# Gated cross-attention and expert block on one core: first inversion split, ids, shares and cells of the second batch reordered

## The chip, the cores and the metric

The kernel runs on one core of a Trainium2 chip. The core has TensorE (PE, matrix products into PSUM), VectorE (DVE), ScalarE (ACT), GpSimd (POOL) and SyncE (SP, which issues DMAs). Each runs its own instruction stream in order and waits for the others on semaphores. The metric is the time of one execution in microseconds (us). Three runs took 621.59, 623.06 and 623.34 us.

## The reference, cut to what matters

`x` is (2, 2048, 512), two batches of 2048 tokens; `ctx` is (2, 154, 512).

```
x = x + tanh(g_xattn) * align(ctx, layernorm(x))      # x1
x = x + tanh(g_ffn)   * experts(layernorm(x1))

align(small, large):            # per batch
    D = euclidean distances (154 x 2048)
    R = cost of the cheapest monotone path through D (dynamic time warping)
    walk back along the path; every cell (i, j) adds small[i] to row j

experts(xf):                    # 8 experts, 512 x 512 each, the best 2 per token
    logits = xf @ gate_w.T
    w, sel = top_k(logits, 2);  w = softmax(w)
    out[n] = sum over the 2 chosen e of  w * (xf[n] @ expert_w[e])
```

## The kernel before, in words

The first 240 us find the path: distances, cost recursion and the walk back, whose end is VectorE work alone. From then on tokens are handled in tiles of 128: 32 tiles, 16 for each batch (`TB` is 16, `t` counts tiles, tile 16 is the first of the second batch).

For each batch the path becomes a 0/1 matrix `prow`, context rows by tokens. `cells(b, half)` makes half of its columns on VectorE: two operations that hold the tick numbers between the limits of a row (line 963), then two compares (line 968); whatever is passed as `between` stands between them. `gated(t)` on TensorE (lines 1606, 1608) multiplies it with small tables for the gate logits of a tile, all 16 tiles into PSUM bank 6. `align(t)` (lines 1621, 1623) multiplies it with the context rows in three bf16 pieces, one PSUM bank per tile, and `add_context(t)` on VectorE (line 985) adds the result to the token tile, which gives x1. The banks go round: alignment of tile 20 needs the bank that `add_context(18)` empties.

`choose(b)` on VectorE (lines 1000 to 1023) takes the two best experts of every token of the batch from bank 6, after all 16 `gated`. `count(b)` on TensorE (lines 1629, 1630) counts them, and `place_choices(b)` on VectorE (from line 1029) gives each of the 4096 choices a slot in 39 tiles (`JT`) that belong to one expert each. The slots are inverted on TensorE, from token by slot to slot by token: `lay_lanes` and `lay_numbers` on VectorE lay two one-hot operands (lines 1068, 1079, 1080), `pads(b)` adds operands for the unused places of the last tile of every expert (lines 1087 to 1097), and `invert(b)` runs 32 matmuls on the first two (line 1643) and 9 on the pads (line 1647). `ids(b)` copies the result into lists of row numbers, for gathers and for the adding DMAs at the end (lines 1126, 1127). `rank(b)` (line 1635) is a small product that `pads` reads. `own_tiles(b)` lays each tile's expert.

ScalarE meanwhile makes `centred(t)`, the x1 rows less their mean, line 1364, which SyncE stores to DRAM as `x2` (line 489) from a ring of four buffers, and `squares(t)`, the sum of squares of the tile, line 1350, with a read of the accumulator. `root(b)` (line 1356) takes the root of the variance for the batch after its 16 squares; `scales(b)` on VectorE (lines 992, 993) needs it, and gives the difference of the logits, from which ScalarE's `shares(b)` takes the exponential (line 1373). Between the two ScalarE copies a set of operands, `members_turned(b)` (line 1368). `lay_shares(b)` on VectorE waits for both (lines 1104 to 1119), `invert_shares(b)` on TensorE (line 1657) inverts the shares to tiles, and `shares_by_tile(b)` on VectorE (line 1132) reads them out.

The expert loop then takes 78 gathered tiles in the order `SEQ`: GpSimd gathers 128 rows (line 637), TensorE transposes them (`turn`, line 1679), ScalarE copies the transposes (`copy_in`, line 1393), TensorE multiplies with the expert's matrix (`expert`, line 1694), ScalarE scales the result (`copy_out`, line 1403) and GpSimd adds it to the output in DRAM (line 650). The first 11 are of batch 0; during them TensorE also runs the alignment of the rest of batch 1, `count(1)`, `rank(1)` and `invert(1)`, and VectorE the whole placement of batch 1. The order on every engine is written out by hand.

Of the kernel before, what the change touches and what calls it, by code (L numbers as in the profile page):

```python
# [5 lines left out]
ALU = mybir.AluOpType  # L6
# [3 lines left out]
F16 = mybir.dt.float16  # L10
# [4 lines left out]
P = 128  # L15
# [4 lines left out]
def flamingo_block(nc, x_d, ctx_d, gx_d, gf_d, gate_d, exp_d, out_d):  # L20
    B, T, C = x_d.shape
    S = ctx_d.shape[1]
    E = gate_d.shape[0]
    CH = C // P
    NT = B * T // P
# [36 lines left out]
    TB = NT // B  # L62
    KT = K * TB
# [22 lines left out]
    with ExitStack() as ctx:  # L86
# [3 lines left out]
        def sem(name):  # L90
            return ctx.enter_context(nc.semaphore(name))
# [270 lines left out]
        s_outside = sem("outside_last_tiles")  # L362
        s_rank = sem("outside_ranked")
        s_oneh = sem("slots_one_hot")
        s_inv = sem("slots_inverted")
        s_ids = sem("tile_ids")
        s_shareh = sem("shares_laid")
# [52 lines left out]
        ALIGNED = [[], [18, 19], [20, 21, 22], [23, 24, 25], [26, 27, 28], [29, 30, 31]]  # L420
        LATE = (4, 5, 4, 5, 4, 5, 6, 4, 5, 6, 4, 5, 6, 4, 5, 6)
        COUNTS = (7, 6)

        def bank(t):
            return RING[t % AR] if t < TB else LATE[t - TB]
# [248 lines left out]
        def _(v):  # L674
# [280 lines left out]
            def cells(b, half, between=lambda: None):  # L955

                n = 2 * (2 * b + half)
                cols = slice(half * HT, (half + 1) * HT)
                low, high = limits[:, half, 0, :, :], limits[:, half, 1, :, :]
                for k in range(2):  # L960
                    if n:
                        v.wait_ge(s_p, n + k - 1)
                    v.tensor_scalar(held[:, k, :], ticks[:, :], low[:, k, b:b + 1], high[:, k, b:b + 1],
                                    ALU.max, ALU.min).then_inc(s_held, 1)
                between()
                for k, rows in enumerate((pmain, prest)):
                    v.wait_ge(s_held, n + k + 1)
                    v.tensor_tensor(rows[:, b, cols], held[:, k, :], ticks[:, :], ALU.is_equal).then_inc(s_p, 1)
# [6 lines left out]
            def lnk(ins):  # L975
                ln[0] += 1
                ins.then_inc(s_gt, 1)
                v.wait_ge(s_gt, ln[0])
# [9 lines left out]
            def scales(b):  # L988

                ts = slice(b * TB, (b + 1) * TB)  # L990
                v.wait_ge(s_sd2, b + 1)
                lnk(v.reciprocal(rs2[:, ts], sd2[:, ts]))
                v.tensor_tensor(sc[:, 0, ts], sc[:, 0, ts], rs2[:, ts], ALU.mult).then_inc(s_dif, 1)
# [76 lines left out]
            def lay_numbers(b):  # L1070

                sets = sets_of(b)
                member = sets[:, SETS - 1, :, :]
                if b:
                    for g in (2, 3):
                        v.wait_ge(s_out[g], 16)
                    v.wait_ge(s_xn2, TB)
                    v.wait_ge(s_sq, TB)
                lnk(v.tensor_tensor(member, spread(partf[:, 0, 0:1], [[0, JT], [1, KT]]), tilen[:, :, :], ALU.is_equal))
                v.tensor_tensor(sets[:, 0, :, :].bitcast(F16), member, spread(numbers[:, 0, 0:1], [[0, JT], [1, KT]]),  # L1080
                                ALU.mult)

            def pads(b):

                v.wait_ge(s_rank, b + 1)
                place_e = padpos[:, 0:E]
                lnk(v.scalar_tensor_tensor(place_e, ntl, -float(P), spread(upto[:, KT - 1:KT], [[KT, E]]),
                                           ALU.mult, ALU.add))
                lnk(v.scalar_tensor_tensor(place_e, place_e, float(P), psum[:, 7, 2 * P:2 * P + E], ALU.add, ALU.add))
                v.tensor_copy(padpos[:, E:LAST], lane[:, :])  # L1090
                lnk(v.scalar_tensor_tensor(place_e, inl[:, :], float(2 * P), place_e, ALU.mult, ALU.add))
                for e in range(LAST):
                    v.tensor_scalar(padhot[:, e, :], stripe[:, :], padpos[:, e:e + 1], None, ALU.is_equal)
                v.tensor_tensor(padset[:, 0:E, :], spread(lastt[:, 0:1], [[1, E], [0, JT]]),
                                spread(tiles[:, 0:1], [[0, E], [1, JT]]), ALU.is_equal)
                lnk(v.tensor_scalar(padset[:, E, :], tiles[:, :], tend[:, E - 1:E], None, ALU.is_ge))
                v.tensor_scalar(padset[:, :, :], padset[:, :, :], lane[:, 0:1], None, ALU.mult).then_inc(s_oneh, 1)

            def lay_shares(b):

                ts = slice(b * TB, (b + 1) * TB)
                sets = sets_of(b)
                v.wait_ge(s_gte, b + 1)
                lnk(v.tensor_scalar(sc[:, 2, ts], sc[:, 1, ts], 1.0, None, ALU.add))
                lnk(v.reciprocal(sc[:, 3, ts], sc[:, 2, ts]))
                lnk(v.scalar_tensor_tensor(share[:, 0, ts], sc[:, 3, ts], tgates[:, 1:2], rs2[:, ts],
                                           ALU.mult, ALU.mult))
                lnk(v.tensor_tensor(share[:, 1, ts], sc[:, 1, ts], share[:, 0, ts], ALU.mult))
                part = share[:, :, ts]
                split = [pieces[:, m, :].rearrange("p (k t) -> p k t", k=K) for m in range(3)]  # L1110
                left = [rests[:, m, :].rearrange("p (k t) -> p k t", k=K) for m in range(2)]
                lnk(v.tensor_copy(split[0], part))
                lnk(v.tensor_tensor(left[0], part, split[0], ALU.subtract))
                lnk(v.tensor_copy(split[1], left[0]))
                lnk(v.tensor_tensor(left[1], left[0], split[1], ALU.subtract))
                lnk(v.tensor_copy(split[2], left[1]))
                v.wait_ge(s_mem, b + 1)
                for m in range(PARTS):
                    ins = v.tensor_tensor(by_slot(sets)[:, :, m, :], members_by_slot(b),
                                          spread(pieces[:, m, 0:1], [[1, KT], [0, JT]]), ALU.mult)  # L1120
                ins.then_inc(s_shareh, 1)

            def ids(b):

                v.wait_ge(s_inv, b + 1)
                v.tensor_copy(gids[:, b, :], psum[:, 7, 0:JT])
                v.tensor_scalar(aids[:, b, :], psum[:, 7, 0:JT], float(b * T), None, ALU.add).then_inc(s_ids, 1)
# [16 lines left out]
                add_context(t)  # L1144
            pads(0)
            own_tiles(0)
            cells(1, 0, lambda: (ids(0), scales(0)))
            cells(1, 1)
            lay_shares(0)
            choose(1, lambda: shares_by_tile(0))  # L1150
            for t in (16, 17):
                add_context(t)
            place_choices(1)
# [20 lines left out]
        def _(act):  # L1174
# [200 lines left out]
            for t in range(10):  # L1375
                centred(t)
                squares(t)
            for t in range(10, TB, 2):
                centred(t)
                centred(t + 1)  # L1380
                if t < TB - 2:
                    squares(10 + (t - 10) // 2)
            for t in range(12, TB):
                squares(t)
            root(0)
            members_turned(0)
# [38 lines left out]
        def _(pe):  # L1425
# [206 lines left out]

            def rank(b):
                pe.wait_ge(s_outside, b + 1)
                nc.tensor.matmul(psum[:, 7, 2 * P:2 * P + E], earlier[:, :], outside[:, :],
                                 start=True, stop=True).then_inc(s_rank, 1)

            def invert(b):

                pe.wait_ge(s_oneh, b + 1)  # L1640
                sets = sets_of(b)
                for i in range(KT):
                    ins = nc.tensor.matmul(psum[:, 7, 0:JT], lanes[:, :, i], sets[:, 0, :, i].bitcast(F16),
                                           start=(i == 0), stop=(i == KT - 1))
                    if i == 0:
                        for e in range(LAST):
                            nc.tensor.matmul(psum[:, 7, 0:JT], padhot[:, e, :], padset[:, e, :],
                                             start=False, stop=False)
                ins.then_inc(s_inv, 1)

            def invert_shares(b):
# [47 lines left out]
            pe.wait_ge(s_x1, TB)  # L1699
            align(16)  # L1700
            align(17)
            for t in range(TB + TB // 2, NT):
                gated(t)
            turn(0)
            for n in range(NSEQ):
                own = owned(n)
                if n + 1 < NSEQ:
                    turn(n + 1)
                expert(n, own)
                if n == 0:  # L1710
                    invert_shares(0)
                if n == 1:
                    count(1)
                if n == 5:
                    invert(1)
                if n < len(ALIGNED):
                    for t in ALIGNED[n]:
                        align(t)
                if n == 2:
                    rank(1)  # L1720
                if n == 10:
                    invert_shares(1)
# [26 lines left out]
```

## Time and profile before

| | |
|---|---|
| median of 3 runs | 623.06 us |
| the profiled execution's own time | 623.45 us |
| its span, first to last instruction | 621.6 us |
| mean granted clock of TensorE, of full | 0.87 |
| TensorE matmul busy | 468.9 us (75%) |
| VectorE busy | 286.5 us (46%) |
| ScalarE busy | 241.4 us (39%) |
| GpSimd busy | 237.3 us (38%) |

The busy shares are means over very different stages. VectorE is nearly full up to 300 us and mostly idle later; TensorE is nearly idle from 172 to 243 us and full from 290 us to the end. The change sits where the one passes into the other, between 270 and 310 us.

### The profile page before, as it was taken

The page shows a single profiled execution, that of the slowest core. Times are in us where ns is not written, and L with a number is a line of the kernel's source. Part 1 is how long each engine was busy: PE and PEld are TensorE (multiplying, and loading weights), DVE is VectorE, ACT ScalarE, POOL GpSimd, SP SyncE. Part 2 cuts the span into 40 slices and gives each one's busy share as a digit, 9 for nine tenths or more (in the row PEclk, how much of TensorE's full clock was granted, in tenths as well). Part 3 has the DMA queues.
Part 4 walks back from the last instruction along what each step waited for, and adds up shares of the span by engine and source line. Part 5 has one row for each costly group of instructions (what it writes and reads, how often), then busy time and mean ns, then how long its engine had stood idle before and what let it go on. Part 6 is the DMA issues. An engine that isn't in the chain of part 4 may idle for free.

```text
span 621.6 us, 7820 instructions
## 1 busy us (share of the span) xinstructions
PE 468.9 (75%) x2118; PEld 276.3 (44%) x2118; DVE 286.5 (46%) x1522; ACT 241.4 (39%) x449; POOL 237.3 (38%) x228
## 2 busy tenths in 40 slices
PE   5999667567100001828999999999999999999994
PEld 5999644344100001315445544444444444444441
DVE  4878989999988885999861400000000000000000
ACT  4477685444400000484779322222222333333331
POOL 5900230000000000004432456676567667666853
PEclk9899877977555555776999999999999999999998
DMA  8962269710051004376878957787787778678875
GB/s 253 391 221 74 70 153 251 188 27 1 0 202 69 1 1 141 124 283 214 272 191 245 283 98 134 136 160 135 120 162 133 134 141 153 113 140 153 147 125 67
DMA packets 56108, 91.78 MB, mean 148 GB/s; under 512 B 19263, under 2 KB 19263, under 8 KB 55907
## 3 DMA queue, kind: packets, MB, share of 16 engines
q0 software_dynamic: 18016, 43.00, 37.5%
q1 hardware_dynamic: 33523, 39.88, 19.5%
q10 hardware_dynamic: 4528, 8.41, 4.2%
q8 instruction: 19, 0.31, 0.2%
q14 instruction: 22, 0.18, 0.1%
HBM read 50.05 MB, written 41.21 MB: 147 GB/s over the span
## 4 chain that ended last, share of the span: by engine, by line
PE 59%; DVE 31%; DMA 4%; issue 4%; ACT 1%; POOL 0%; SPq 0%; POOLq 0%; ACTq 0%; DVEq 0%
PE psum L1694 40%; DVE met L923 5%; PE psum L1679 5%; PE psum L1472 5%; DVE waves L836 5%; DVE tokens L926 3%; DVE tokens L861 3%; DVE shf L827 2%; PE psum L1459 2%; DVE tokens L839 2%; DVE tokens L985 2%; PE psum L1621 2%; DVE tokens L830 2%; DMA ar<-in_ctx_dram 1%; DVE waves L826 1%
## 5 line engine op out<-in xcount | busy, mean ns | idle before, releaser
L1694 PE MATMUL psum<-big,tokens 128*128 x624 | 280.6, 593 | 0.3 <-ACT tokens L1393 0.3
L1694 PEld LDWEIGHTS psum<-big,tokens 128*128 128x128 f32 x624 | 112.5, 190 | 112.9 <-issue 112.9
L637 POOL DMA_INDIRECT tokens<-x_rows,gather_ids x78 | 79.1, 1014 | 45.7 <-issue 21.3
L650 POOL DMA_INDIRECT out_dram<-work,add_ids x40 | 63.2, 1580 | 53.6 <-DMA out_dram<-work,add_ids 26.3
L650 POOL DMA_INDIRECT out_dram<-prow,add_ids x38 | 59.9, 1577 | 45.9 <-DMA out_dram<-prow,add_ids 11.9
L657 POOL DMA_DIRECT2D out_dram<-tokens x2 | 1.8, 912 | 172.3 <-DVE tokens L985 172.3
L1403 ACT ACTIVATE work<-psum,tile_shares 128x512 f32<-128x512 f32 x40 | 27.5, 686 | 99.4 <-PE psum L1694 93.5
L1403 ACT ACTIVATE prow<-psum,tile_shares 128x512 f32<-128x512 f32 x38 | 26.1, 686 | 92.1 <-PE psum L1694 92.1
L1364 ACT ACTIVATE stage<-tokens,nm 128x512 f32<-128x512 f32 x32 | 21.7, 713 | 96.8 <-DVE tokens L985 96.7
L1679 PEld LDWEIGHTS psum<-ident,tokens 128*128 128x128 f32 x312 | 39.0, 143 | 39.0 <-issue 33.7
L1590 PE MATMUL psum<-side,work 128*128 128x2 f32 x8 | 1.9, 356 | 70.9 <-DVE work L944 70.9
L1393 ACT COPY tokens<-psum 128x512 f32<-128x512 f32 x78 | 45.0, 579 | 12.2 <-PE psum L1679 12.2
L1679 PE MATMUL psum<-ident,tokens 128*128 128x128 f32 x312 | 47.3, 275 | 1.3 <-DMA tokens<-x_rows,gather_ids 1.3
L836 DVE TENSOR_TENSOR_SCAN waves<-waves,shf,tokens 128x65 f32<-128x65 f32 x108 | 37.9, 351 | 2.4 <-DMA tokens<-dist_rows 2.4
L1472 PE MATMUL psum<-aT,big 128*128 128x162 f32 x256 | 37.7, 305 | 0.0
L1472 PEld LDWEIGHTS psum<-aT,big 128*128 128x128 f32 x256 | 36.6, 194 | 0.0
L1590 PEld LDWEIGHTS psum<-side,work 128*128 128x128 f32 x8 | 1.8, 327 | 71.0 <-DVE work L944 71.0
L923 DVE SCALAR_TENSOR_TENSOR met<-tokens 128x70 bf16<-128x70 bf16 x108 | 31.5, 292 | 3.8
L1621 PE MATMUL psum<-sm,prow 128*128 128x512 bf16 x96 | 29.1, 415 | 1.4 <-DVE tokens L985 1.4
L826 DVE TENSOR_TENSOR waves<-waves 128x64 f32<-128x64 f32 x108 | 24.3, 225 | 0.1
L985 DVE SCALAR_TENSOR_TENSOR tokens<-psum,tgates,tokens 128x512 f32<-128x512 f32 x32 | 22.3, 743 | 2.5 <-PE psum L1623 2.1
L1350 ACT ACTIVATE aT<-tokens,nm 128x512 f32<-128x512 f32 x32 | 23.0, 719 | 1.1
(320 smaller groups left out, 614.2 us busy)
## 6 DMA issues: line engine op xcount, KB each, us to landing
tokens<-in_x_dram SPq DMA_DIRECT2D x16, 1024.0 KB, 11.1
stage<-in_L_ffn_expert_w_dram ACTq DMA_DIRECT2D x8, 1024.0 KB, 6.2
x_rows<-stage SPq DMA_DIRECT2D x32, 256.0 KB, 2.5
out_dram<-tokens SPq DMA_DIRECT2D x6, 1024.0 KB, 8.1
tokens<-dist_rows SPq DMA_DIRECT2D x52, 64.0 KB, 2.2
dist_rows<-work SPq DMA_DIRECT2D x16, 160.0 KB, 2.0
out_dram<-tokens POOLq DMA_DIRECT2D x2, 1024.0 KB, 5.1
dist_rows<-prow SPq DMA_DIRECT2D x5, 256.0 KB, 10.4
```

Of the source, the lines that this page charges most:

```text
L637: pool.indirect_dma_start(out=xin[:, n % UX, :], out_offset=None, in_=x2_d[b][:, :], in_offset=bass.IndirectOffsetOnAxis(ap=gids[:, b, j:j ...
L650: pool.indirect_dma_start(out=out_d.rearrange("b t c -> (b t) c"), in_=yout(n), in_offset=None, out_offset=bass.IndirectOffsetOnAxis(ap=ai ...
L826: v.tensor_tensor(mring[:, s % 3, 1:W1], up[:, 0:W], up[:, 1:W1], ALU.min).then_inc(s_min, 1)
L836: v.tensor_tensor_scan(own, mring[:, s % 3, :], dring[:, s // CS % DR, s % CS, :], shf[:, s % 2, 0:1], ALU.min, ALU.add).then_inc(s_row, 1)
L923: v.scalar_tensor_tensor(met[:, :], words[:, s + 1, :], words[:, s + 1, TW - 1:TW], itab[:, s, :], ALU.is_equal, ALU.mult, accum_out=words ...
L985: v.scalar_tensor_tensor(x[:, t, :], psum[:, bank(t), :], tgates[:, 0:1], x[:, t, :], ALU.mult, ALU.add).then_inc(s_x1, 1)
L1393: nc.scalar.copy(xinT[:, n % UX, :, :].rearrange("p c n -> p (c n)"), psum[:, n % UP, :]).then_inc(s_yc, 1)
L1403: nc.scalar.mul(yout(n), psum[:, UP + n % UP, :], scale[:, b, j:j + 1]).then_inc(s_ye, 1)
L1472: ins = nc.tensor.matmul(to, xT[:, c, at + k * P:at + (k + 1) * P], aT[:, b, c, :], start=(c == 0), stop=(c == CH - 1))
L1621: nc.tensor.matmul(psum[:, bank(t), :], pmain[:, b, cols], sm[:, b, j, 0:C], start=(j == 0), stop=False)
L1679: ins = nc.tensor.transpose(psum[:, n % UP, c * P:(c + 1) * P], xin[:, n % UX, c * P:(c + 1) * P], ident[:, :])
L1694: ins = nc.tensor.matmul(psum[:, UP + n % UP, :], xinT[:, n % UX, c, :], expT[:, bass.ds(own, 1), c, :].rearrange("p o d -> p (o d)"), sta ...
```

## The change

- `invert(b)`: the 32 matmuls on the slot numbers come first, on a new semaphore that `lay_numbers` raises; the 9 on the pads come last, in batch 0 behind their own wait.
- `rank(0)` writes to bank 6 beside the gating results instead of to bank 7.
- VectorE: `ids(0)` ahead of `cells(1, 0)` instead of inside it; `lay_shares(0)` ahead of `cells(1, 1)`; `shares_by_tile(0)` ahead of `choose(1)` instead of inside it.
- ScalarE: `centred` of tiles 10 to 15, then `squares` of tiles 10 to 15, instead of the two interleaved.
- TensorE: `gated` of tiles 24 to 31 behind expert 0 and `invert_shares(0)` instead of ahead of the first transposes.

```diff
+        RANKS = ((6, 3 * G * TB), (7, 2 * P))
...
                 v.tensor_tensor(sets[:, 0, :, :].bitcast(F16), member, spread(numbers[:, 0, 0:1], [[0, JT], [1, KT]]),
-                                ALU.mult)
+                                ALU.mult).then_inc(s_numl, 1)
...
             pads(0)
             own_tiles(0)
-            cells(1, 0, lambda: (ids(0), scales(0)))
+            ids(0)
+            cells(1, 0, lambda: scales(0))
+            lay_shares(0)
             cells(1, 1)
-            lay_shares(0)
-            choose(1, lambda: shares_by_tile(0))
+            shares_by_tile(0)
+            choose(1)
...
-            for t in range(10, TB, 2):
+            for t in range(10, TB):
                 centred(t)
-                centred(t + 1)
-                if t < TB - 2:
-                    squares(10 + (t - 10) // 2)
-            for t in range(12, TB):
+            for t in range(10, TB):
                 squares(t)
...
             def invert(b):
 
-                pe.wait_ge(s_oneh, b + 1)
+                pe.wait_ge(s_numl, b + 1)
+                if b:
+                    pe.wait_ge(s_oneh, b + 1)
                 sets = sets_of(b)
                 for i in range(KT):
-                    ins = nc.tensor.matmul(psum[:, 7, 0:JT], lanes[:, :, i], sets[:, 0, :, i].bitcast(F16),
-                                           start=(i == 0), stop=(i == KT - 1))
-                    if i == 0:
-                        for e in range(LAST):
-                            nc.tensor.matmul(psum[:, 7, 0:JT], padhot[:, e, :], padset[:, e, :],
-                                             start=False, stop=False)
+                    nc.tensor.matmul(psum[:, 7, 0:JT], lanes[:, :, i], sets[:, 0, :, i].bitcast(F16),
+                                     start=(i == 0), stop=False)
+                if b == 0:
+                    pe.wait_ge(s_oneh, 1)
+                for e in range(LAST):
+                    ins = nc.tensor.matmul(psum[:, 7, 0:JT], padhot[:, e, :], padset[:, e, :],
+                                           start=False, stop=(e == LAST - 1))
                 ins.then_inc(s_inv, 1)
...
             align(16)
             align(17)
-            for t in range(TB + TB // 2, NT):
-                gated(t)
             turn(0)
             for n in range(NSEQ):
...
                 if n == 0:
                     invert_shares(0)
+                    for t in range(TB + TB // 2, NT):
+                        gated(t)
```

On VectorE, from the owners of batch 0 (`am`, `owners`) on, the order before was this; `work` are the held ticks and `prow` the cells, `rs` and `sc` belong to `scales(0)`, and the `sc` row at the end begins `lay_shares(0)`.

```order
L1062 CAST owners<-am 1x39
L963 TENSOR_SCALAR work<-ticks,row_limits 128x1024 x2
L1126 CAST gather_ids<-psum 128x39
L1127 TENSOR_SCALAR add_ids<-psum 128x39
L992 RECIPROCAL rs<-aux 128x16
L993 TENSOR_TENSOR sc<-sc,rs 128x16
L968 TENSOR_TENSOR prow<-work,ticks 128x1024 x2
L963 TENSOR_SCALAR work<-ticks,row_limits 128x1024 x2
L968 TENSOR_TENSOR prow<-work,ticks 128x1024 x2
L1104 TENSOR_SCALAR sc<-sc 128x16
```

It is now as follows; the lines below the edits have moved by 2.

```order
L1064 CAST owners<-am 1x39
L1128 CAST gather_ids<-psum 128x39
L1129 TENSOR_SCALAR add_ids<-psum 128x39
L965 TENSOR_SCALAR work<-ticks,row_limits 128x1024 x2
L994 RECIPROCAL rs<-aux 128x16
L995 TENSOR_TENSOR sc<-sc,rs 128x16
L970 TENSOR_TENSOR prow<-work,ticks 128x1024 x2
L1106 TENSOR_SCALAR sc<-sc 128x16
```

The ids have moved ahead of the held ticks, and the second pair of held ticks and cells no longer stands between the first and the shares. Where it stands now shows further down the same engine, at the end of `lay_shares(0)` (`ar`, `tokens`) and the start of `choose(1)` (`ar<-psum`, line 1002 now):

```order
L1118 CAST ar<-ar 128x32
L1121 TENSOR_TENSOR tokens<-tokens,ar 128x32x39 x3
L965 TENSOR_SCALAR work<-ticks,row_limits 128x1024 x2
L970 TENSOR_TENSOR prow<-work,ticks 128x1024 x2
L1134 TENSOR_REDUCE tile_shares<-psum 128x39
L1002 TENSOR_REDUCE ar<-psum 128x144
```

Between the shares and `choose(1)` there are now the second half of the cells and the tile shares. On TensorE, around the end of expert 0 (`big` are the experts' matrices) and the inversion of the shares (32 matmuls), the order before was

```order
L1694 MATMUL psum<-big,tokens 128x512
L1657 MATMUL psum<-tokens,stage 128x117 x32
L1687 TENSOR_LOAD owners
L1687 ISA x2
L1679 MATMUL psum<-ident,tokens 128x128 x4
```

and it is now, with the first two of the eight moved tiles:

```order
L1698 MATMUL psum<-big,tokens 128x512
L1661 MATMUL psum<-tokens,stage 128x117 x32
L1607 MATMUL psum<-sm,prow 128x27
L1609 MATMUL psum<-srs,prow 128x9
L1607 MATMUL psum<-sm,prow 128x27
```

The gating of tiles 24 to 31 follows the shares' inversion, where the next tile's transposes stood.

## Rows read from the trace of the kernel before

**Rows 1.** The page's chain that ended last: shares of the span by engine.

```profile
PE 59%; DVE 31%; DMA 4%; issue 4%; ACT 1%; POOL 0%; SPq 0%; POOLq 0%; ACTq 0%; DVEq 0%
```

**Rows 2.** TensorE's waits, 268 to 350 us: total us, times, longest us.

```profile
PE psum L1643 <- DVE waves L1097: 9.1, 1, 9.1
```

**Rows 3.** The chain in order of time, 280 to 400 us: start us, us, what.

```profile
286.09 1.28 PE psum L1621 x3
287.37 0.43 PE psum L1623
...
288.20 0.97 PE psum L1679 x4
...
289.92 3.69 PE psum L1694 x8
293.61 2.01 PE psum L1657 x32
...
305.55 0.66 DVE tokens L985
```

**Rows 4.** Timeline of VectorE: start us, us, instruction, [idle before, releaser].

```profile
271.96 4.04 DVE L985 SCALAR_TENSOR_TENSOR tokens<-psum,tgates,tokens 128x512 f32<-128x512 f32 x6
...
280.26 0.98 DVE L963 TENSOR_SCALAR work<-ticks,row_limits 128x1024 f16<-128x1024 f16 x2
281.80 0.20 DVE L1126 CAST gather_ids<-psum 128x39 uint32<-128x39 f32 x1 [0.55 <-PE psum L1643]
...
282.39 1.33 DVE L968 TENSOR_TENSOR prow<-work,ticks 128x1024 bf16<-128x1024 f16 x2
...
285.80 0.29 DVE L1104 TENSOR_SCALAR sc<-sc 128x16 f32<-128x16 f32 x1
...
292.10 0.60 DVE L1000 TENSOR_REDUCE ar<-psum 128x144 f32<-128x432 f32 x1
...
295.73 0.28 DVE L1132 TENSOR_REDUCE tile_shares<-psum 128x39 f32<-128x117 f32 x1 [0.28 <-PE psum L1657]
...
299.76 0.69 DVE L1029 TENSOR_TENSOR_SCAN am<-aT,psum 128x256 f32<-128x256 f32 x1 [0.56 <-PE psum L1630]
```

**Rows 5.** Timeline of ScalarE, squares to exponential of batch 0.

```profile
277.88 0.71 ACT L1350 ACTIVATE aT<-tokens,nm 128x512 f32<-128x512 f32 x1
...
280.60 0.74 ACT L1350 ACTIVATE aT<-tokens,nm 128x512 f32<-128x512 f32 x1
...
281.47 0.31 ACT L1356 ACTIVATE aux<-inverse_roots,eps 128x16 f32<-128x16 f32 x1
281.69 2.32 ACT L1368 COPY tokens<-tokens 128x1248 bf16<-128x1248 bf16 x1
284.02 1.28 ACT L1373 ACT_TABLE_LOAD   x1
285.32 0.21 ACT L1373 ACTIVATE sc<-sc 128x16 f32<-128x16 f32 x1
```

**Rows 6.** Timeline of TensorE at the inversion and at two waits.

```profile
279.15 0.48 PE L1647 MATMUL psum<-waves 128*128 128x39 f16 x9
279.47 2.29 PE L1643 MATMUL psum<-tokens,stage 128*128 128x39 f16 x31
...
306.26 0.82 PE L1621 MATMUL psum<-sm,prow 128*128 128x512 bf16 x3 [0.92 <-DVE tokens L985]
...
347.83 0.66 PE L1679 MATMUL psum<-ident,tokens 128*128 128x128 f32 x4 [1.35 <-DMA tokens<-x_rows,gather_ids]
```

**Rows 7.** Windows of 1 us: sum, five engines' busy us, PEclk, DMA share, GB/s.

```profile
280.00:281.00 1.00, 1.00 (x18) 1.00 (x17) 0.97 (x4) 0.91 (x3) 0.00 (x0) 0.50 0.07 16
...
289.00:290.00 1.00, 0.69 (x6) 0.46 (x4) 1.00 (x2) 0.81 (x2) 0.57 (x1) 0.97 0.81 307
```

**Rows 8.** GpSimd's first gather; stores of x1 rows (line 489), issue to landing.

```profile
282.39 1.06 POOL L637 DMA_INDIRECT tokens<-x_rows,gather_ids  x1 [14.32 <-DVE add_ids L1127]
...
DMA to landing us min/median/max: 2.0/2.5/8.4
```

More of the change, by code:

```diff
@@ L364, in flamingo_block @@
         s_oneh = sem("slots_one_hot")
+        s_numl = sem("slot_numbers_laid")
         s_inv = sem("slots_inverted")
@@ L1088, in pads @@
                                            ALU.mult, ALU.add))
-                lnk(v.scalar_tensor_tensor(place_e, place_e, float(P), psum[:, 7, 2 * P:2 * P + E], ALU.add, ALU.add))
+                lnk(v.scalar_tensor_tensor(place_e, place_e, float(P), psum[:, RANKS[b][0], RANKS[b][1]:RANKS[b][1] + E], ALU.add, ALU.add))
                 v.tensor_copy(padpos[:, E:LAST], lane[:, :])
@@ L1634, in rank @@
                 pe.wait_ge(s_outside, b + 1)
-                nc.tensor.matmul(psum[:, 7, 2 * P:2 * P + E], earlier[:, :], outside[:, :],
+                nc.tensor.matmul(psum[:, RANKS[b][0], RANKS[b][1]:RANKS[b][1] + E], earlier[:, :], outside[:, :],
                                  start=True, stop=True).then_inc(s_rank, 1)
             def invert(b):
-                pe.wait_ge(s_oneh, b + 1)
+                pe.wait_ge(s_numl, b + 1)
+                if b:
+                    pe.wait_ge(s_oneh, b + 1)
                 sets = sets_of(b)
                 for i in range(KT):
-                    ins = nc.tensor.matmul(psum[:, 7, 0:JT], lanes[:, :, i], sets[:, 0, :, i].bitcast(F16),
-                                           start=(i == 0), stop=(i == KT - 1))
-                    if i == 0:
-                        for e in range(LAST):
-                            nc.tensor.matmul(psum[:, 7, 0:JT], padhot[:, e, :], padset[:, e, :],
-                                             start=False, stop=False)
+                    nc.tensor.matmul(psum[:, 7, 0:JT], lanes[:, :, i], sets[:, 0, :, i].bitcast(F16),
[5 more added lines that the diff above has]
+                                           start=False, stop=(e == LAST - 1))
                 ins.then_inc(s_inv, 1)
```

## The prediction

> **What bounds the kernel now.** I read the page's chain of waits first: TensorE is 59% of it, VectorE 31% [rows 1]. Then TensorE's own waits from 268 to 350 us: the longest, 9.1 us, is for the pads of the first inversion [rows 2]; the others of note are for the path cells of the second batch, 0.92 us for a token sum and 1.35 us for a gathered tile, which ends at 347.83 us [rows 6]. Behind that one TensorE has no wait up to its last matmul. So the change is worth what it moves TensorE's work at 347.83, and what sets that time comes down the chain in order of time [rows 3]: alignment of tiles 16 and 17, the transposes of gathered tile 0, expert 0, the inversion of the shares, and at 305.55 the sum of token tile 18 on VectorE. The last one matters most. Tile 20's alignment takes the PSUM bank that `add_context(18)` empties, and VectorE came to that sum only after `choose(1)`, the sums of 16 and 17 and `place_choices(1)`. There is no slack there: TensorE stood 0.92 us for it [rows 6].
>
> **The change, part by part.**
>
> *1. Inversion split (TensorE).* The 32 matmuls of the first inversion now need only the slot numbers, laid when the sums of tiles 10 to 15 begin, 271.96 [rows 4]; the 9 on the pads come last. Before, one ran, then the 9 in 0.48 us, then 31 in 2.29 us, to 281.76 [rows 6]. Now the 32 lie beside `add_context(10..15)`, and behind the pads (laid at 279.0) only the 9 remain. The inversion is ready at about 279.6 and VectorE finds it done when it comes to `ids(0)`.
>
> *2. `ids(0)` ahead of the held cells.* VectorE ends the owners at 280.26, does both ids in 0.31 us (281.80 to the end at 282.11 before), and holds the cells for 1.0 us, to 281.55. Its idle 0.55 us ahead of the ids goes [rows 4]. The gather of tile 0 starts at 280.57 + 0.28 = 280.85 instead of 282.39 [rows 8]. TensorE never waited for that gather, so on the path this brings nothing.
>
> *3. Six centred tiles first, six squares last (ScalarE).* The root of the x1 variance, on which `scales(0)` waits, comes after the last square. Before, two of the six squares of tiles 10 to 15 lay between centred tiles, and the last four ran at (280.60 - 277.88) / 3 = 0.907 us each, since each waits for the accumulator of the one before; the root started at 281.47 [rows 5]. Now all six do: 5.44 us. They start when `centred(15)` ends. That one waits for `add_context(15)`, done at 271.96 + 4.04 = 276.00, and for the store of tile 11, whose row buffer it takes: tile 11 is centred by about 274.05, and a store lands 2.0 us at the least and 2.5 us in the median after its issue [rows 8]. So it starts between 276.1 and 276.7, ends at 276.7 to 277.3, and the root starts at 282.2 to 282.8. I take 282.25, nearest to the row of VectorE's own pace: 0.8 us later than before.
>
> *4. Cells of the second batch, first half.* VectorE has held them by 281.55 and stands for the root, which ends at 282.25 + 0.31 = 282.56. From the reciprocal to the end of both compares it took 1.70 us (282.02 to 282.39, and 1.33) [rows 4]; so the cells are done at 284.35 instead of 283.72. Gating of tiles 16 to 23 starts 0.63 us late, and alignment of 17 ends at 287.80 + 0.63 = 288.43 [rows 3]. The 2.2 us of inversion taken off the path buy nothing: the squares on ScalarE take its place.
>
> *5. Gating of tiles 24 to 31 behind expert 0.* It filled the 0.40 us between alignment 17 and the transposes of tile 0 (287.80 to 288.20). So these start at 288.43, 0.23 us later than before, and expert 0 at about 290.15 instead of 289.92. Its 3.69 us and the 2.01 us of the share inversion [rows 3] end at 295.85.
>
> *6. `lay_shares(0)` ahead of `cells(1,1)`.* It waits for ScalarE's exponentials. Behind the root lie there the copy of the members (281.69 to 284.02, 2.33 us), a table load of 1.28 and the exponential, 0.21 [rows 5]; so they come at 286.3. Before, VectorE worked on the second half of the cells meanwhile; that cover is gone, and it is idle from 284.35 to 286.35. Then the shares take their 6.3 us (285.80 to 292.10) [rows 4]: laid at about 292.7. TensorE comes for them at 293.84, so the 2.0 us cost nothing there. `cells(1,1)` (1.0 and 1.3 us, 0.1 of it overlapped) ends at 294.9; TensorE runs the last gating matmuls from 295.85 to 296.3.
>
> *7. What is late next: `choose(1)`.* It reads all 16 gating results of the batch. Before, it started at 292.10, during expert 0, right behind the shares. Now it starts at 296.4, behind expert 0, the share inversion and the gating: 4.3 us later. From its start to the end of `add_context(18)` VectorE took 306.21 - 292.10 = 14.11 us [rows 3, 4]. Of this 0.48 us goes (the tile shares with the 0.28 us wait for them now come ahead), and so does the 0.56 us wait for the counting matmuls [rows 4], since TensorE does `count(1)` while VectorE adds 16 and 17. Left: 13.07 us. Tile 18 is added at 309.5 and the alignment of tile 20 starts at 309.52 instead of 306.26: **+3.26 us**. TensorE's own work up to there would be done by about 308, after new waits of about 1.3 us before the count and 0.5 us before alignment 18; so VectorE's chain decides and leaves 1.4 us idle before tile 20.
>
> *8. Behind that.* From tile 20 to the gather wait TensorE has the same work. The gather wait itself (1.35 us) ends with the stores of the second batch's rows, which follow ScalarE's `centred(31)`, which follows TensorE's alignment of 31: it moves along and absorbs nothing. The pads last in the second inversion: 41 matmuls as before. `rank(0)` in another PSUM bank: nothing.
>
> The sum against the profiled execution: 623.45 + 3.3 = 626.7, of which the span is 621.6 + 3.3 = 624.9. The median of the runs shown, 623.06, is 0.4 below that execution, so I forecast **626.4**.
>
> **The clock.** The granted clock was at its low level (0.50, 1.2 of 2.4 GHz) while the inversion ran at 280, and at the high one from 289, in the first transposes [rows 7]. At the low level an alignment took 1.28 + 0.43 = 1.71 us [rows 3], its first three matmuls 1.3 against 0.7 to 0.8 us later on [rows 6]. I expect the same two slow alignments, 16 and 17. If the rise comes only inside expert 0, up to 1 us is added, with half of expert 0's 3.4 us slow as the far bound of 1.7; if a little earlier than before, 0.5 us is saved.
> The Trainium skill (TensorE: Matmul & The Clock Gate, Part 1: The HAM clock gate) has it that activity releases the throttle and idleness brings it back. By that rule the inversion, moved to 272 right behind the alignments, might keep the engine at full clock. The trace speaks against it here: an inversion of the same length was followed by gating and alignment at 0.50. As a gain the rule is rival C.
>
> **Rivals.**
>
> *B, not slower.* The chain of VectorE behind `choose(1)` is hidden by experts 1 and 2, and the root is not late. Then the cells end at 281.55 + 1.70 = 283.25 (0.47 us earlier), the gating is out of the way (0.40), and TensorE's order alone counts: -0.9 us, 622.2. It decides from the point where VectorE has more than 4 us of slack between `choose(1)` and tile 18. Against it: the 0.92 us wait says that the slack is below zero. For it: only that TensorE was busy for all but 0.92 us of that stretch.
>
> *C, the clock stays high* through alignment 16 and 17. It saves 2 x 0.85 and half of the 0.97 us of transposes, 2.2 us, and leaves +1.1: 624.2. Against it: between the early inversion and the cells TensorE does nothing in some 10 us but the 9 pad matmuls.
>
> *D, later still.* The store of tile 11 lands late (the slowest of its line took 8.4 us [rows 8]), or the clock rises inside expert 0, or ScalarE, which now meets `centred(16)` only at 302.3 and has the second lane numbers behind it, holds up the copies that the experts need. +3.3 and 1.5 to 2 more: 628.2.
>
> **Chances.** A, the forecast, 0.67, with its own range 625.4 to 627.4 (the root 0.7 to 1.3 us late, the clock term 0.5 us either way, half the spread of the runs, 621.59 to 623.34). B 0.11, C 0.08, D 0.14. The measurement can tell some 0.3%, 1.9 us, from no change. Slower by more than that: nearly all of A, and D: 0.80. Within it: most of B and C, 0.15. Faster needs a gain of 1.9 us, twice that of B: 0.05. The range leaves out B and the far end of D: 623.5 to 628.4.
>
> **What would show it.** The 32 matmuls at 272; the root at 282.2 or later, VectorE waiting for it and then 2 us for the exponentials; expert 0 within 0.5 us of 290.1; `choose(1)` at about 296.4; new waits of TensorE before the count and alignment 18, and one of over 1 us before tile 20, which starts 3.3 us later; the gather wait still near 1.35 us. I am wrong if tile 20's alignment does not wait, if expert 0 starts more than 2 us earlier, or if the gather wait shrinks to nothing.

## The result and the profile after

The changed kernel took 626.32 us (median of 5 runs, 624.19 to 628.69), the kernel before 622.86 us beside it (median of 5, 621.59 to 623.34): 1.006 times as long, 95% interval 1.003 to 1.0089. It is slower by 3.46 us. The profiled execution took 626.32 us with a span of 624.6 us, against 621.6 us.

The two traces are laid over each other where the sums of tiles 10 to 15 begin on VectorE: 271.96 us before [rows 4], 272.00 us after. That matters, because in the traces of this study this point lies anywhere between 269.54 and 273.84 us, though nothing that VectorE does ahead of it was edited. Below, "after the origin" means this point of the same trace.

The chain of waits by engine, first row of the page's part on it:

```profile
PE 58%; DVE 33%; DMA 3%; issue 3%; ACT 2%; POOL 0%; SPq 0%; ACTq 0%; DVEq 0%; POOLq 0%
```

VectorE's share rose from 31% to 33% and ScalarE's from 1% to 2% [rows 1]. TensorE's timeline (start us, us, instruction, idle before and its releaser) shows where:

```profile
272.13 2.39 PE L1646 MATMUL psum<-tokens,stage 128*128 128x39 f16 x32 [2.09 <-DVE tokens L1082]
...
279.11 0.48 PE L1651 MATMUL psum<-waves 128*128 128x39 f16 x9 [4.59 <-DVE waves L1099]
...
285.40 0.20 PE L1607 MATMUL psum<-sm,prow 128*128 128x27 bf16 x1 [5.80 <-DVE prow L970]
...
287.51 1.32 PE L1622 MATMUL psum<-sm,prow 128*128 128x512 bf16 x3
...
290.26 3.70 PE L1698 MATMUL psum<-big,tokens 128*128 x8 [0.32 <-ACT tokens L1394]
...
301.54 0.28 PE L1630 MATMUL psum<-hot,earlier 128*128 128x256 bf16 x1 [0.75 <-DVE hot L1016]
...
302.64 0.60 PE L1622 MATMUL psum<-sm,prow 128*128 128x512 bf16 x2 [0.71 <-DVE tokens L987]
...
309.65 0.82 PE L1622 MATMUL psum<-sm,prow 128*128 128x512 bf16 x3 [1.46 <-DVE tokens L987]
...
350.10 0.66 PE L1683 MATMUL psum<-ident,tokens 128*128 128x128 f32 x4 [0.25 <-DMA tokens<-x_rows,gather_ids]
...
354.60 2.25 PE L1661 MATMUL psum<-tokens,stage 128*128 128x117 bf16 x32 [0.41 <-DVE tokens L1121]
```

The inversion is done at 279.6 us, yet the first matmul of the second batch's gating still waits, 5.80 us, for the cells. Tile 20 (309.65) waits 1.46 us for a token sum instead of 0.92 [rows 6], and the late gathered tile waits only 0.25 us instead of 1.35 [rows 6]. VectorE's timeline says what it did with the time:

```profile
280.31 0.18 DVE L1128 CAST gather_ids<-psum 128x39 uint32<-128x39 f32 x1
...
280.52 0.98 DVE L965 TENSOR_SCALAR work<-ticks,row_limits 128x1024 f16<-128x1024 f16 x2
283.68 0.25 DVE L994 RECIPROCAL rs<-aux 128x16 f32<-128x16 f32 x1 [2.18 <-ACT aux L1360]
...
287.44 0.17 DVE L1106 TENSOR_SCALAR sc<-sc 128x16 f32<-128x16 f32 x1 [2.10 <-ACT sc L1377]
...
296.06 0.28 DVE L1134 TENSOR_REDUCE tile_shares<-psum 128x39 f32<-128x117 f32 x1 [0.23 <-PE psum L1661]
296.48 0.61 DVE L1002 TENSOR_REDUCE ar<-psum 128x144 f32<-128x432 f32 x1
```

The 0.55 us wait of [rows 4] became one of 2.18 us for the root, and 2.10 us for the exponentials joined it. `choose(1)` begins at 296.48 instead of 292.10 [rows 4]. ScalarE's timeline has the cause of the first:

```profile
276.44 0.72 ACT L1368 ACTIVATE stage<-tokens,nm 128x512 f32<-128x512 f32 x1 [0.97 <-DMA x_rows<-stage]
277.33 0.72 ACT L1368 ACTIVATE stage<-tokens,nm 128x512 f32<-128x512 f32 x1 [0.17 <-issue]
277.96 0.71 ACT L1354 ACTIVATE aT<-tokens,nm 128x512 f32<-128x512 f32 x1
...
283.34 0.31 ACT L1360 ACTIVATE aux<-inverse_roots,eps 128x16 f32<-128x16 f32 x1
```

Two causes meet here. All six squares now lie behind `centred(15)`, two more than before, at 0.91 us each. And `centred(14)` stood 0.97 us for the store of tile 10. So the six squares began at 277.96 and the root at 283.34, against 281.47 before [rows 5].

### The profile page after: what moved, and what is told of

Read it like the earlier page. It is cut to its first block, busy times and chain, and to the rows that moved or that the text cites. A ratio compares the mean times of both kernels' runs of the same rounds, so it can differ in the third digit from the quotient of the medians.

```text
span 624.6 us, 7808 instructions
## 1 busy us (share of the span) xinstructions
PE 468.7 (75%) x2106; PEld 277.8 (44%) x2118; DVE 286.6 (46%) x1522; ACT 242.1 (39%) x449; POOL 238.1 (38%) x228
## 4 chain that ended last, share of the span: by engine, by line
PE 58%; DVE 33%; DMA 3%; issue 3%; ACT 2%; POOL 0%; SPq 0%; ACTq 0%; DVEq 0%; POOLq 0%
PE psum L1698 41%; DVE met L925 5%; PE psum L1683 5%; PE psum L1473 5%; DVE waves L838 5%; DVE tokens L928 3%; DVE tokens L863 3%; DVE shf L829 2%; PE psum L1460 2%; DVE tokens L841 2%; DVE tokens L832 2%; PE psum L1622 2%; DMA ar<-in_ctx_dram 1%; DVE tokens L987 1%; DVE waves L828 1%
## 5 line engine op out<-in xcount | busy, mean ns | idle before, releaser
L1698 PE MATMUL psum<-big,tokens 128*128 x624 | 280.6, 593 | 0.3 <-ACT tokens L1394 0.3
L1622 PE MATMUL psum<-sm,prow 128*128 128x512 bf16 x90 | 27.2, 407 | 3.5 <-DVE tokens L987 2.9
```

Of the source, the lines that this page charges most:

```text
L1622: nc.tensor.matmul(psum[:, bank(t), :], pmain[:, b, cols], sm[:, b, j, 0:C], start=(j == 0), stop=False)
L1698: ins = nc.tensor.matmul(psum[:, UP + n % UP, :], xinT[:, n % UX, c, :], expT[:, bass.ds(own, 1), c, :].rearrange("p o d -> p (o d)"), sta ...
```

## The experiments

Every kernel was timed against the kernel before, in three sets of four kernels (e1 to e4; e5, e6, e7 and e10; e11 to e14), each with its own runs of the kernel before on the same chip (medians 623.73, 623.87 and 623.35 us). The runs of one kernel spread by 2 to 8 us, and the start of the stretch of interest alone moves by 4.3 us from trace to trace, so steps are read from one trace each, in us after the origin. "Gather ends" is where the transposes of gathered tile 11 begin, the tile that TensorE waits for in [rows 6]:

```
                                gating 16  expert 0  choose(1)  tile 20  gather   last matmul
                                starts     starts    starts     aligned  ends     ends
before                          11.82      17.96     20.14      34.30    75.87    341.00
after                           13.40      18.26     24.48      37.65    78.10    343.88
e1 gating late only             11.83      17.46     23.76      37.00    77.45    343.22
e2 after, ScalarE as before     11.56      17.05     23.21      36.28    76.74    342.49
e3 split and ids only           11.55      17.28     20.03      33.77    75.41    340.52
e4 e3 + squares last            13.26      19.06     21.49      35.34    77.00    342.15
e5 e3 + scales after cells      10.76      17.82     20.12      34.57    76.68    343.61
e6 after + sums in placing      13.57      18.34     24.65      36.21    77.06    342.82
e7 e5 + sums in placing         10.76      17.84     20.13      33.50    75.74    340.92
e10 before + sums in placing    11.83      17.97     20.16      33.25    75.19    340.34
e11 e3 + sums in placing        11.58      17.72     20.05      32.98    75.41    342.24
e12 e11 + twelve ahead          11.56      17.71     20.03      32.95    -        341.71
e13 e11 + nine idle matmuls     11.61      15.99     19.87      32.10    73.93    339.08
e14 before + twelve ahead       11.83      17.62     20.15      34.08    -        342.99
```

**One part done alone: the gating of tiles 24 to 31.** On the kernel before:

```diff
-            for t in range(TB + TB // 2, NT):
-                gated(t)
             turn(0)
...
                     invert_shares(0)
+                    for t in range(TB + TB // 2, NT):
+                        gated(t)
```

> One part alone: the gating of tiles 24 to 31 moved behind the inversion of the shares, all else as before. My theory (the decision chain of VectorE has no slack behind choose(1)): choose(1) starts at about 296.0 instead of 292.1, TensorE then waits over 1 us for the sum of tile 18, and the time is +2.6 to +3.4 us, about 626. The rival (the late root and the cells behind it cost the time, not the gating): -0.4 to 0, about 622.7.

Measured: 624.49 us, ratio 1.0013 (1.0 to 1.0026), some 0.8 us slower (0 to 1.6), where 2.6 to 3.4 had been expected. In the trace tile 20 is 2.70 us late and the last matmul 2.22 us. VectorE's timeline of this kernel, around `choose(1)`:

```profile
287.27 4.20 DVE L1119 TENSOR_TENSOR tokens<-tokens,ar 128x1248 bf16<-128x1248 bf16 x3
294.99 0.61 DVE L1000 TENSOR_REDUCE ar<-psum 128x144 f32<-128x432 f32 x1 [3.52 <-PE psum L1608]
```

VectorE had the shares laid and then stood 3.52 us for the last gating matmul. With this one edit step 7 of the prediction is there: `choose(1)` 3.6 us late, tile 20 2.7 us late. The size in the time was missed, and is less than the trace has it.

**One part undone: the squares.** The changed kernel with ScalarE's old order:

```diff
-            for t in range(10, TB):
-                centred(t)
-            for t in range(10, TB):
-                squares(t)
+            for t in range(10, TB, 2):
+                centred(t)
+                centred(t + 1)
+                if t < TB - 2:
+                    squares(10 + (t - 10) // 2)
+            for t in range(12, TB):
+                squares(t)
```

> The changed kernel with ScalarE's order as before (squares 10 and 11 between the centred tiles). Root back to about 281.5 from 283.3, cells of the first half at 283.5, expert 0 at about 289.1. My theory: choose(1) still starts only behind expert 0, the share inversion and the gating, at about 295.4, so +2.0 to +2.6 us against the kernel before, about 625.2. The rival (the late root carries the loss): within 0.5 us of the kernel before, 623.

Measured: 624.62 us, 1.0016 (1.0005 to 1.0028), 0.3 to 1.7 us slower than the kernel before, less than the 2.0 to 2.6 expected. Tile 20 comes 1.37 us earlier than in the changed kernel (36.28 for 37.65), the last matmul 1.39. So the late root is worth about 1.4 of the 3.35 us at tile 20. ScalarE never stood for a store here: its root began at 9.49 after the origin, against 11.34 in the changed kernel and 9.51 before. In all three traces with the squares last it stood, 0.97 us in the changed kernel, 0.81 in e4 and 1.13 in e6, and the root began at 11.34, 11.19 and 11.50.

**The parts without the late gating.** e3 keeps the inversion split and the ids first, with ScalarE's, TensorE's and VectorE's further order as before:

```diff
-            cells(1, 0, lambda: (ids(0), scales(0)))
+            ids(0)
+            cells(1, 0, lambda: scales(0))
```

> Only the split inversion and ids(0) ahead of the held cells; ScalarE, shares, cells and gating as before. My theory: VectorE's 0.55 us wait for the inversion goes and little more, since it then meets the root: -0.2 to -0.8 us, about 622.4. The rival (the inversion's 2.2 us were on the path and come off it): -2 us or more, under 621.

e4 is e3 with the squares last.

> As the split-and-ids kernel, with the six squares behind the six centred tiles as in the changed kernel; shares, cells and gating as before. My theory: the root comes 1.8 us later and VectorE, which has no slack, moves with it: choose(1) at about 293.5, +1.0 to +1.6 us against the kernel before, about 624.2. The rival (a late root hides behind the second half of the cells): as the split-and-ids kernel within 0.3 us.

Measured: e3 622.83 us, 0.9982 (0.9964 to 0.9999); e4 624.95 us, 1.001 (0.9991 to 1.0029). e3 came out as expected in size. VectorE no longer waits for the inversion there, and meets the root instead:

```profile
281.87 0.25 DVE L994 RECIPROCAL rs<-aux 128x16 f32<-128x16 f32 x1 [0.33 <-ACT aux L1359]
```

The split gains 0.53 us at tile 20 and 0.48 at the end: the root was right behind the inversion. The squares last turn this into 1.04 us later than before at tile 20 and 1.15 at the end (e4).

**Taking the root out of the way.** e5 is e3 with the reciprocal of the root behind the whole first half of the cells:

```diff
-            cells(1, 0, lambda: scales(0))
+            cells(1, 0)
+            scales(0)
```

> The split-and-ids kernel with scales(0) behind the two compares of cells(1,0) instead of ahead of them, so that the cells don't wait for the root. Counted from the end of lay_numbers(0): gating of tile 16 at 10.8 us instead of 11.8 in the kernel before, tile 20 at 33.5 instead of 34.3, last matmul at 340.2 instead of 341.0; -0.8 us. The rival (VectorE's chain has slack, TensorE's own order counts): -1.0 at the gating and at tile 20 alike, with the wait before tile 20 gone.

Measured: 624.94 us, 1.0018 (1.0001 to 1.0034): a miss, slower where a gain of 0.8 us was expected. The gating did start 1.06 us earlier than before, but expert 0 only 0.14 us, and `choose(1)` not at all. GpSimd's timeline of this kernel:

```profile
281.18 2.15 POOL L639 DMA_INDIRECT tokens<-x_rows,gather_ids  x1 [13.38 <-ACT aT L1354]
283.64 2.08 POOL L639 DMA_INDIRECT tokens<-x_rows,gather_ids  x1 [0.30 <-issue]
286.02 0.94 POOL L639 DMA_INDIRECT tokens<-x_rows,gather_ids  x1 [0.30 <-issue]
```

and TensorE's, at the transposes of gathered tile 0, and at tile 11:

```profile
288.18 0.66 PE L1686 MATMUL psum<-ident,tokens 128*128 128x128 f32 x4 [0.43 <-DMA tokens<-x_rows,gather_ids]
...
348.36 0.66 PE L1686 MATMUL psum<-ident,tokens 128*128 128x128 f32 x4 [1.92 <-DMA tokens<-x_rows,gather_ids]
348.85 5.30 PE L1701 MATMUL psum<-big,tokens 128*128 x8
```

Two gathers took 2.1 us of GpSimd instead of 1.06 [rows 8], and TensorE stood for the first of them. VectorE ran holds and compares beside them almost without a gap; but so it did in the kernel before, from 282.39 to 285.87, where the gathers took 1.06, 1.04 and 0.99 us. What made these two longer stays open. Later the expert of tile 11 took 5.30 us instead of 3.60, at a granted clock of 0.50 from 349 to 352 us.

**What waits at tile 20.** If `add_context(18)` comes too late, it can go ahead of the rest of `place_choices(1)`:

```diff
-            place_choices(1)
-            for t in (18, 19):
-                add_context(t)
+            place_choices(1, lambda: [add_context(t) for t in (18, 19)])
```

with the call of the function behind the line that computes `tbeg`. On the changed kernel:

> The changed kernel with add_context(18) and (19) inside place_choices(1), behind its tbeg, instead of behind it. If TensorE's wait of 1.46 us before tile 20 is VectorE's chain, it goes: tile 20 at 36.2 us from the end of lay_numbers(0) instead of 37.65, and the last matmul 0.3 to 1.1 us earlier than in the changed kernel, at 342.8 to 343.6. The rival (the wait hides another that takes its place, PSUM or the count): tile 20 at 37.5 or later.

on e5:

> The scales-after-cells kernel with the sums of tiles 18 and 19 inside place_choices(1) as well. Tile 20 without a wait at 32.4 us instead of 34.3 in the kernel before, tile 22 at 34.4 instead of 36.0, last matmul at 339.3 instead of 341.0: -1.7 us, about 622.0 where the kernel before takes 623.7. The rival (the later gather wait, 1.35 us before, grows by what is gained): last matmul at 340.2, no better than the kernel it is made from.

on the kernel before:

> The kernel before with only the sums of tiles 18 and 19 moved inside place_choices(1). Theory: the 0.92 us wait before tile 20 goes, tile 20 at 33.4 us from the end of lay_numbers(0), last matmul at 340.1 instead of 341.0: -0.9 us. The rival (absorbed by the gather wait): 341.0, no change.

and on e3:

> The split-and-ids kernel (-0.5 us in its trace) with the sums of tiles 18 and 19 inside place_choices(1) (-0.7 us in its trace). Both act on VectorE's one chain at different places, so they should add: last matmul at 339.8 us from the end of lay_numbers(0) instead of 341.0, -1.2 us. The rival (the gather wait of tile 11 takes back what is gained): 340.5.

Measured: e6 626.3 us, 1.0044 (1.0028 to 1.006); e7 624.15, 1.0002 (0.9984 to 1.0019); e10 622.88, 0.9991 (0.9974 to 1.0007); e11 623.09, 0.9985 (0.9965 to 1.0004). The wait ahead of tile 20 is gone in all four. In the changed kernel that gives 1.06 us in the trace, as expected, so the wait was real and no longer the only one: tile 22 waits 0.26 us. The time of e6 does not show this gain. In the kernel before it gives 0.66 us in the trace (0.9 expected) and nothing that the times can tell. e7 and e11 missed: their last matmuls ended at 340.92 and 342.24, later than even their rivals had it. e11 had 0.46 us in hand at the gather wait and then lost more than that:

```profile
345.87 1.12 PE L1684 MATMUL psum<-ident,tokens 128*128 128x128 f32 x4 [2.14 <-DMA tokens<-x_rows,gather_ids]
```

The clock was 0.50 from 346 to 349 us; these transposes took 1.12 us instead of 0.66 and the expert behind them 4.86 instead of 3.60.

What is gained at tile 20 is not all kept at the gather wait. Against the kernel before, e3 has 0.53 us at tile 20 and 0.46 at the gather's end, e10 1.05 and 0.68, e11 1.32 and 0.46, e13 (below) 2.20 and 1.94. The wait there is 1.43, 1.57, 2.14 and 1.49 us instead of 1.35: the tile's rows do come sooner, but not by the whole gain.

**Moving the gather wait.** The first tile of the second batch is sent to the experts one place later (`AHEAD = 12`, the lags kept), on e11 and on the kernel before:

> The kernel with the split, the ids and the sums, with 12 instead of 11 gathered tiles of the first batch ahead of the second batch's first. TensorE's wait of 1.4 to 1.6 us for the first gather of the second batch is then covered by another expert: it goes, and the last matmul comes another 1.4 us earlier, at 338.4 instead of 341.0 in the kernel before; -2.6 us. The rival (the wait moves to the shares of the second batch or to the DMAs that add): -1.2 us at most.

> The kernel before with 12 instead of 11 tiles of the first batch ahead, alone. The gather wait of 1.35 us goes: last matmul at 339.7 us from the end of lay_numbers(0) instead of 341.0, -1.3 us. The rival (the wait is moved, not covered): 341.0.

Measured: e12 622.78 us, 0.999 (0.9966 to 1.0013); e14 624.23, 1.0002 (0.9987 to 1.0016). Both missed. The last matmul ended at 341.71 in e12 (338.4 expected) and at 342.99 in e14 (339.7 expected), there 2.0 us later than in the kernel before. The gather wait at that tile is gone, but in e14 the shares' inversion takes it over in part:

```profile
350.84 2.25 PE L1657 MATMUL psum<-tokens,stage 128*128 128x117 bf16 x32 [0.87 <-DVE tokens L1119]
```

Later gathered tiles wait too, 0.47 and 1.74 us in e14, 0.40 and 1.10 in e12.

**The clock.** e11 with nine matmuls of 512 columns behind the inversion, whose result nothing reads:

```diff
             invert(0)
+            pe.wait_ge(s_x1, TB)
+            for _ in range(9):
+                nc.tensor.matmul(psum[:, 0, :], earlier[:, :], sm[:, 0, 0, 0:C], start=True, stop=True)
```

> The kernel with the split, the ids and the sums, with 9 idle matmuls of 512 columns on TensorE behind the first inversion, whose result nobody reads, in the 3.9 us in which it waits for the cells. If they bring the clock up before the alignment of 16 and 17, each of these takes 0.87 instead of 1.71 us and expert 0 starts 1 to 2 us earlier; but VectorE's chain from the shares on is the bound, so the last matmul gains only its 0.5 us wait for the count: 339.3 against 339.8. The rival (TensorE's order is the bound there): -1.5 us or more against the kernel without them.

Measured: 621.84 us, 0.9973 (0.9955 to 0.9991): the lowest median of all, 1.5 us under the kernel before in its set and 1.25 under e11. The windows of e13 and then of e3, which has no such matmuls (PEclk is the third number from the end):

```profile
283.00:284.00 1.00, 1.00 (x18) 0.53 (x16) 1.00 (x3) 0.98 (x2) 0.70 (x2) 0.50 0.68 229
284.00:285.00 1.00, 1.00 (x6) 0.43 (x5) 1.00 (x3) 0.77 (x2) 0.69 (x2) 0.95 0.68 213
285.00:286.00 1.00, 1.00 (x21) 0.76 (x20) 0.86 (x5) 0.00 (x0) 0.81 (x1) 1.00 0.67 176
```

```profile
286.00:287.00 1.00, 1.00 (x4) 0.31 (x3) 0.86 (x5) 0.00 (x0) 0.69 (x2) 0.50 0.54 102
287.00:288.00 1.00, 1.00 (x19) 0.72 (x18) 0.83 (x6) 0.00 (x0) 0.30 (x1) 0.51 0.62 223
288.00:289.00 1.00, 1.00 (x10) 0.74 (x8) 1.00 (x1) 0.40 (x1) 0.17 (x1) 1.00 0.80 166
```

The nine matmuls took 4.01 us, from 278.65, in a stretch in which TensorE has nothing else to do, and were done before the cells were. The clock rose at about 284 us, inside the first alignment, instead of in the transposes: about 12.9 us after the origin, against 15.9 in e3. Expert 0 began 1.29 us earlier than in e3 and 1.73 earlier than in e11. Then VectorE bounds: TensorE waited for the shares, which it had not done in e11, and `choose(1)` began only 0.18 us earlier. The last matmul ended at 339.08, where 339.3 was expected. Of the 3.2 us by which that is ahead of e11, 1.7 are the slow transposes and expert of e11 behind its gather wait. TensorE's timeline of e13:

```profile
278.65 4.01 PE L1678 MATMUL psum<-sm,earlier 128*128 128x512 bf16 x9
...
283.28 1.20 PE L1623 MATMUL psum<-sm,prow 128*128 128x512 bf16 x3
...
291.23 2.24 PE L1662 MATMUL psum<-tokens,stage 128*128 128x117 bf16 x32 [0.33 <-DVE tokens L1122]
```

## Why the prediction was right, step by step

626.4 us was forecast and 626.32 measured. The mechanism and most sizes held; two errors cancelled, and that the figures agree to 0.1 us is luck. The forecast for the profiled execution was 626.7, from which 0.4 was taken for the median; the execution took 626.32 and was itself the median.

*Steps 1 and 2* held: the 32 matmuls at 272.13, the inversion ready at 279.6, nothing of the gather on the path. The gather itself began at 281.81, 0.58 us earlier and not 1.54: the ids were ready at 280.6, and the profile puts its wait down to ScalarE's squares; whether those or the last store held it is not shown. e3 shows the gain of the split, 0.5 us, when nothing else is moved; step 2's "nothing" counted against a root made late by step 3.

*Step 3* named the right store mechanism and mis-sized it. The root began 1.83 us later after the origin, not 0.8, and outside the 0.7 to 1.3 us of the forecast's own range. Squares took 5.38 us, as worked out (5.44); it was their start that was late, 277.96 instead of at most 277.3. The store that held ScalarE was tile 10's, 2.79 us in the chain, and `centred(14)` stood for it, ahead of the `centred(15)` that the step looked at.

*Step 4*, in consequence: cells done at 285.35 (forecast 284.35; its own terms, 282.56 and 1.70, add up to 284.26).

*The clock term* gave this back. The clock was at the high level again in the second alignment, not in the transposes: window of 1 us, changed kernel,

```profile
288.00:289.00 1.00, 1.00 (x5) 0.48 (x4) 0.86 (x5) 0.00 (x0) 0.00 (x0) 0.73 0.67 197
```

so alignment 17 took 1.38 us from 287.51 to the transposes at 288.89, instead of 1.71. With that and with faster transposes expert 0 started at 290.26 (*step 5*: 290.15), though the cells were 1.0 us later than forecast. Two terms of opposite sign met there; the range held both.

*Step 6* held: 2.10 us for the exponentials (2.0 forecast), shares laid at 293.7 (292.7 and the 1.0 us of step 4), just before TensorE came for them at 293.79.

*Step 7* held to some 0.1 us: `choose(1)` at 296.48 (296.4), tile 20 at 309.65 (309.52). The waits were 0.75, 0.71 and 1.46 us (1.3, 0.5 and 1.4). e1 shows it as a cause by itself. The 3.35 us after the origin divide by experiment: 1.4 are the late root (e2), and e2's remaining 2.0 are the late gating, 2.7 (e1), less the gain of the rest, 0.5 (e3), and 0.2 that are not accounted for. No run moves the shares ahead of the second half of the cells alone; in the changed kernel VectorE was through with both at 295.83, before the last gating matmul ended at 296.45, so `choose(1)` did not start late for them.

*Step 8* failed in part. The gather wait was to move along whole; it shrank from 1.35 to 0.25 us, close to the "shrinks to nothing" that the prediction had named as a sign against itself. Its reason was that the gather follows the stores and ScalarE's `centred(31)`. ScalarE was done with that one 3.4 us later: its next instruction starts at 335.46 before and 338.84 after. But the gather, 4.77 us behind that before (340.23), came 3.36 us behind it after (342.20). The two or three stores issued in that stretch landed in a median 2.1 us instead of 3.6; why they did is not shown. That gave back 1.1 us; 0.41 came on top as a wait for the second batch's shares, and some 0.2 elsewhere. The late gating goes with both: in all four traces that have it (the changed kernel, e1, e2, e6) the gather wait is 0.22 to 0.25 us and that for the shares 0.40 to 0.43, while the kernel before has 1.35 and none. The last matmul ended 2.88 us later after the origin, not 3.3. The median moved by 3.46 us, which the interval (1.9 to 5.5 us) does not tell from either.

*The rivals.* B (chain hidden) is refuted by e1 and by the 1.46 us wait. C (clock kept by the early inversion) is refuted: the inversion itself ran at full clock (1.00 at 272), but the clock fell just before 275 and was 0.50 until 288. Its price was real, as e13 shows, 1.3 to 1.7 us at expert 0. D did not occur: the store put `centred(15)` at 277.33, 0.6 us behind the far end of step 3 and not more, and the clock rose earlier.

*Open*: by the times the parts do not add up as they do by the traces. e1 lost 0.8 us in time (interval 0 to 1.6) and 2.2 in its trace, and e2 lost 1.0 and 1.5, while the whole change lost 3.5 and 2.9. Nothing here explains it; one trace is one execution, and the medians come from different sets.

## What to carry to other kernels

Work that fills a gap on one engine may be what another engine's next long chain waits for: price a move by the start of that chain (here 4.3 us late for a 0.4 us gap filled). Taking away the longest wait (9.1 us) was worth 0.5 us, because the root on ScalarE was due right behind it (e3), and with the root out of the way the first gathered tile was (e5); list the second and third arrival before a wait is cut. Where TensorE is to resume heavy work at a known time behind a pause, a few matmuls that nobody reads, placed in the pause, are worth a try: here e13 is the only version whose whole interval lies more than 0.5 us below the kernel before. They were tried on e11 alone, and part of that gain may be e11's own.

## What the hardware did that was not expected

- A gather's instruction on GpSimd took 0.94 to 1.06 us in most places, and 2.15 and 2.08 us beside VectorE's 16-bit compares and holds in e5 (2.18 and 2.09 in e7). The Trainium skill (SBUF — State Buffer, Who interferes with whom) has it that VectorE's two-port modes shut GpSimd out of a shared port pair for a whole instruction. The rows do not bear this out as the cause here: in the kernel before, the first three gathers lay beside the same compares and holds and took 1.06, 1.04 and 0.99 us. The fifth gather, beside the product of the shares (line 1119), took 2.21 us there and 0.98 in e11. No run tests it apart.
- A wait of TensorE of about 2 us was followed by the low clock in two traces and not in a third. In e5 it waited 1.92 us, then the clock was 0.50 for three microseconds and the expert took 1.7 us longer. In e11 it waited 2.14 us, and the transposes and the expert together took 1.7 us longer. In e7 it waited 1.97 us, the clock stayed at 1.00 and the expert took 3.60 us. e5 and e7 were 0.9 us apart at that tile and ended 2.7 us apart.
- In the kernel before, the clock stayed at 0.50 through the 2.7 us of the inversion [rows 6, 7] and rose at 289 us, in the transposes. In e13 nine matmuls of 512 columns followed the end of the inversion and ran to 282.66, and the clock rose at about 284 us.
- Squares in a row on ScalarE start 0.91 us apart though each takes 0.72, in the changed kernel as before [rows 5]; a read of the accumulator, 0.19 us, lies between two of them.
